# Attention score products of two neighbouring heads in two row tiles of the TensorE array

## What is computed

```python
q, k_text, v_text = hidden @ Wq, text @ Wk, text @ Wv
logits = einsum('bhqd,bhkd->bhqk', q_h, k_h) * scale          # 77 text tokens
text_out = softmax(logits) @ v_h
scores = einsum('bhqd,bhkd->bhqk', q_h, ip_k_h) * scale       # 179 ip tokens
fused = scores + 0.5 * sem[:, None]                           # sem: one for all heads
ip_out = (softmax(fused) * spatial_mask) @ ip_v_h
out = (text_out + ip_out) @ Wout + bout + residual
```

## Time and profile before

| | |
|---|---|
| median of 3 runs | 1717.98 us (1716.74 to 1719.43) |
| the profiled execution | 1715.15 us |
| its span, first to last instruction | 1713.0 us |
| granted TensorE clock, mean | 0.988 |
| PE busy | 1625.4 us, 95% |
| DVE busy | 1380.9 us, 81% |
| ACT busy | 1033.4 us, 60% |
| POOL busy | 833.2 us, 49% |

### The profile page before, as it was taken

One profiled execution on the slowest core, in us unless ns is written; L12 is line 12 of the kernel. 1 busy time (PEld: TensorE's weight loads), 2 busy tenths in 40 slices (PEclk: granted clock), 3 DMA queues, 4 the chain that ended last, 5 costly groups with the idle time before them and its releaser, 6 DMA issues.

```text
span 1713.0 us, 42882 instructions
## 1 busy us (share of the span) xinstructions
PE 1625.4 (95%) x14568; PEld 1440.6 (84%) x14568; DVE 1380.9 (81%) x3630; ACT 1033.4 (60%) x2204; POOL 833.2 (49%) x691
## 2 busy tenths in 40 slices
PE   4899999999999999999999999999999999999986
PEld 4788888888888888877888888898889888898965
DVE  4577777777777777866889988999889999999884
ACT  3366665666665666655666666666666666666652
POOL 4422222222222222333577667766677566756663
PEclk9999999999999999998999999999999999999998
DMA  7433343334333433543233323332333223332211
GB/s 204 99 105 109 116 122 112 120 117 122 115 116 114 121 113 117 152 118 90 82 96 100 99 65 87 104 97 81 85 98 103 80 72 97 108 87 55 83 29 41
DMA packets 185985, 172.72 MB, mean 101 GB/s; under 512 B 25760, under 2 KB 185770, under 8 KB 185770
## 3 DMA queue, kind: packets, MB, share of 16 engines
q1 hardware_dynamic: 185770, 169.98, 34.1%
HBM read 110.17 MB, written 57.76 MB: 98 GB/s over the span
## 4 chain that ended last, share of the span: by engine, by line
PE 78%; DVE 9%; ACT 4%; issue 4%; POOL 2%; SPq 2%; DMA 1%; DVEq 0%; ACTq 0%; POOLq 0%
PE MISC L101 25%; PE GP L101 16%; PE NAT L226 9%; PE TR L256 7%; PE PV L303 4%; PE PV L287 4%; PE PV L284 2%; PE PV L306 2%; PE MISC L335 2%; DVE PM L819 2%; DVE TA L806 1%; PE MISC L476 1%; ACT PVS L541 1%; PE PV L244 1%; ACT PH L534 1%
## 5 line engine op out<-in xcount | busy, mean ns | idle before, releaser
L970 POOL TENSOR_TENSOR ZS<-ZP 128x256 f32<-128x256 f32 x267 | 267.2, 1001 | 230.7 <-DVE ZP L813 230.6
L527 ACT ACTIVATE P<-TA 128x512 f32<-128x512 f32 x320 | 202.0, 631 | 269.4 <-DVE TA L806 269.0
L226 PE MATMUL NAT<-KS,QS 65*128 65x256 f32 x1280 | 295.6, 313 | 9.5 <-DMA KS<-qk_parts 5.7
L256 PE MATMUL TR<-QS,KS 69*128 69x256 f32 (+1 forms) x1280 | 272.0, 294 | 0.3 <-DVE TA L806 0.2
L975 POOL TENSOR_TENSOR PARTS<-QKF,PARTS 112x512 fp32r<-112x512 f32 (+3 forms) x96 | 126.7, 1320 | 293.6 <-ACT PARTS L555 293.6
L226 PEld LDWEIGHTS NAT<-KS,QS 65*128 65x128 f32 x1280 | 203.0, 191 | 73.5 <-issue 63.5
L101 PE MATMUL GP<-PH,GH 128*128 128x256 f32 (+1 forms) x960 | 244.2, 285 | 15.9 <-DVE ZP L813 15.9
L813 DVE TENSOR_TENSOR ZP<-GP,PM 128x512 f32<-128x512 f32 x320 | 219.2, 685 | 46.5 <-PE GP L101 43.8
L819 DVE SCALAR_TENSOR_TENSOR PM<-P,PH 128x512 f32<-128x512 f32 x320 | 252.3, 788 | 0.0
L797 DVE TENSOR_REDUCE MX<-NAT 128x2 f32<-128x504 f32 x320 | 216.0, 675 | 33.2 <-PE NAT L226 30.4
L101 PE MATMUL GP<-PH,GL 128*128 128x256 f32 (+1 forms) x960 | 240.9, 279 | 0.0
(11 more groups left out here) (279 smaller groups left out, 3959.9 us busy)
## 6 DMA issues: line engine op xcount, KB each, us to landing
QS<-qk_parts SPq DMA_DIRECT2D x480, 64.0 KB
KS<-qk_parts SPq DMA_DIRECT2D x480, 64.0 KB
qk_parts<-PARTS SPq DMA_DIRECT2D x128, 224.0 KB, 2.8
CT<-in_ctx_t SPq DMA_DIRECT2D x32, 512.0 KB, 4.2
qk_parts<-PARTS SPq DMA_DIRECT2D x64, 192.0 KB, 2.4
QS<-NH SPq DMA_DIRECT2D x480, 4.0 KB
XT<-in_x_t SPq DMA_DIRECT2D x48, 112.0 KB, 2.2
XT<-x_t SPq DMA_DIRECT2D x48, 112.0 KB, 2.3
```

Of the source, the lines that this page charges most:

```text
L226: ins = e.matmul(NAT[s % 2][:, i * T:(i + 1) * T], QS[0:KQ, h, i * 128:(i + 1) * 128], KS[0:KQ, h, :], start=True, stop=True)
L256: ins = e.matmul(TR[s % 2][:, i * S:(i + 1) * S], KS[0:w, h, i * 128:(i + 1) * 128], QS[0:w, h, :], start=True, stop=True)
L527: e.activation(P[:, s % NP, :], TA[:, s % 2, :], ACT.Exp, scale=SCALE).then_inc(q["exp"], 1)
L970: e.tensor_tensor(ZS[s % NZ][:, :], ZP[:, s % 2, 0:S], ZP[:, s % 2, S:2 * S], ALU.add).then_inc(q["zs"], 1)
```

## The change

It is one rewrite of how scores are stacked, multiplied and read:

- The stacks lose their zero rows and are 48 rows high (`KM`); even heads stand in rows 0 to 47 of QS and KS, odd heads in rows 64 to 111 (`UP`), the rows of maxima and ones right behind each. Both are 10 pairs wide for each of two batches.
- NAT and TR are one tile each of two banks; a pair of heads is multiplied by four matmuls into each, by turns in the lower and the upper row tile (64 rows by 128 columns of the array). On PE, TR and NAT of a pair stand next to each other at the end of every second slot, NAT 10 slots ahead instead of 11.
- DVE reads a pair's maxima in one reduction (in layer 0 the four passes of the fused term stay), TA, PM, P and PH are made for two heads in one instruction.
- `spill` writes the parts to DRAM in the order of the stack, three times 16 rows for Q and for K; `stack` fetches half a batch with four DMAs. The rows of maxima go to DRAM with one DMA and from there to QS with two.
- The offsets of other work, and the rule by which the ring hands out banks, are changed: each taker says how long it will hold its bank, and the bank that comes free first is taken.

```diff
-KQ, KM = 65, 65
-STACKS = 2 * len(Q_PARTS)
-LEAD = 11
+KM, UP = 48, 64
+LEAD = 10
+HP = H // 2
...
+STACK = ((-1, 3), (7, 11))
...
 def mrows(g):
 
-    return 64 * (g // 2 + 1) if g < G1 else 32 * G1 + 32 * ((g - G1) // 2 + 1)
+    return 32 * (g // 2 + 1)
 
...
-    QS, KS = sb("QS", [TRK0, H, S], F32R), sb("KS", [TRK0, H, T], F32R)
+    QS, KS = sb("QS", [UP + TRK0, 2 * HP, S], F32R), sb("KS", [UP + TRK0, 2 * HP, T], F32R)
...
-    NAT = [bank(f"NAT{k}") for k in range(2)]
-    TR = [bank(f"TR{k}") for k in range(2)]
+    NAT, TR = (ctx.enter_context(nc.psum_tensor(n, [128, 1024], F32)) for n in ("NAT", "TR"))
...
+    def pair_at(t, off, lo=0, hi=2 * S1):
+
+        return t - off if (t - off) % 2 == 0 and lo <= t - off < hi else None
+
+    def slot_of(s):
+
+        return s // H % 2 * HP + s % H // 2
...
-            s = t + LEAD
-            if 0 <= s < 2 * S1:
-                b, h = divmod(s, H)
-                if s == 0:
-                    e.wait_ge(q["w_rest"], 3 * 16)
-                    e.wait_ge(q["clear"], 4)
-                    e.wait_ge(q["clear_q"], 2)
-                if h % HG == 0:
-                    e.wait_ge(q[f"stack{h // HG}"], stacked(b + 1))
-                if s >= 2:
-                    e.wait_ge(q["mx"], s - 1)
-                for i in range(2):
-                    ins = e.matmul(NAT[s % 2][:, i * T:(i + 1) * T], QS[0:KQ, h, i * 128:(i + 1) * 128],
-                                   KS[0:KQ, h, :], start=True, stop=True)
-                ins.then_inc(q["nat"], 1)
...
+            s = pair_at(t, 0)
+            if s is not None:
+                b, h, k = s // H, s % H, slot_of(s)
+                if h % HG == 0:
+                    e.wait_ge(q[f"mrow{s // HG % 2}"], mrows(s // HG))
+                    if s == 0:
+                        e.wait_ge(q["sel"], 32)
+                if s:
+                    e.wait_ge(q["sum"] if s <= S1 else q["exp"], s // 2)
+                w = TRK0 if b < B else TRK1
+                for i in range(2):
+                    for r in (0, UP):
+                        ins = e.matmul(TR[:, 8 * r + i * S:8 * r + (i + 1) * S], KS[r:r + w, k, i * 128:(i + 1) * 128],
+                                       QS[r:r + w, k, :], start=True, stop=True)
+                ins.then_inc(q["tr"], 1)
+            s = pair_at(t, -LEAD)
+            if s is not None:
+                b, h, k = s // H, s % H, slot_of(s)
+                if s == 0:
+                    e.wait_ge(q["w_rest"], 3 * 16)
+                if h % HP == 0:
+                    e.wait_ge(q[f"stack{h // HP}"], stacked(h // HP, b + 1))
+                if s:
+                    e.wait_ge(q["mx"], s // 2)
+                for i in range(2):
+                    for r in (0, UP):
+                        ins = e.matmul(NAT[:, 8 * r + i * T:8 * r + (i + 1) * T], QS[r:r + KM, k, i * 128:(i + 1) * 128],
+                                       KS[r:r + KM, k, :], start=True, stop=True)
+                ins.then_inc(q["nat"], 1)
 
...
+            s = pair_at(t, 2, 0, S1)
+            if s is not None:
                 if s == 0:
                     e.wait_ge(q["once"], 2)
                     e.wait_ge(q["norm"], 1)
                     e.wait_ge(q["vall_out"], 16)
                 if s >= NP and s % HG == 0:
                     e.wait_ge(q["pv"], (s - NP) // HG + 1)
-                if s < S1:
-                    e.wait_ge(q["sum"], s + 1)
-                    e.activation(P[:, s % NP, :], TA[:, s % 2, :], ACT.Exp, scale=SCALE).then_inc(q["exp"], 1)
-                else:
-                    e.wait_ge(q["tr"], s + 1)
-                    e.activation(P[:, s % NP, :], TR[s % 2][:, :], ACT.Exp, scale=SCALE).then_inc(q["exp"], 1)
-                    if s - S1 >= NS:
-                        e.wait_ge(q["gp"], s - S1 - NS + 1)
-                    e.wait_ge(q["exp"], s + 1)
-                    e.copy(PH[:, s % NS, :], P[:, s % NP, :]).then_inc(q["ph"], 1)
-            for off, lo, hi, width in ((HG + 1, 0, G1, 2 * S), (HG + 3, G1, 2 * G1, S)):
+                e.wait_ge(q["sum"], s // 2 + 1)
+                e.activation(P[:, s % NP:s % NP + 2, :], TA[:, :, :], ACT.Exp, scale=SCALE).then_inc(q["exp"], 1)
+            s = pair_at(t, 1, S1)
+            if s is not None:
+                if s % HG == 0:
+                    e.wait_ge(q["pv"], (s - NP) // HG + 1)
+                e.wait_ge(q["tr"], s // 2 + 1)
+                e.activation(P[:, s % NP:s % NP + 2, :], TR[:, :].rearrange("p (r n) -> p r n", r=2), ACT.Exp, scale=SCALE).then_inc(q["exp"], 1)
+                k = (s - S1) % NS
+                if s - S1 >= NS:
+                    e.wait_ge(q["gp"], s - S1 - NS + 2)
+                e.wait_ge(q["exp"], s // 2 + 1)
+                e.copy(PH[:, k:k + 2, :], P[:, s % NP:s % NP + 2, :]).then_inc(q["ph"], 1)
+            for off, lo, hi, width in ((HG + 2, 0, G1, 2 * S), (HG + 4, G1, 2 * G1, S)):
                 g = due_group(t, off, lo, hi)
...
+            s = pair_at(t, 1, 0, S1)
+            if s is not None:
+                b, h = divmod(s, H)
+                if h == 0:
+                    e.wait_ge(q["st"], b + 1)
+                if s:
+                    e.wait_ge(q["exp"], s // 2)
+                e.wait_ge(q["tr"], s // 2 + 1)
+                e.tensor_tensor(TA[:, :, :], TR[:, :].rearrange("p (r n) -> p r n", r=2),
+                                ST[:, b % 2, :].unsqueeze(1).broadcast_to([128, 2, 2 * S]), ALU.add).then_inc(q["sum"], 1)
+            s = t - 3 - S1
+            if 0 <= s < S1:
+                if s >= 2:
+                    e.wait_ge(q["zs"], s - 1)
+                e.wait_ge(q["pm"], s // 2 + 1)
+                e.wait_ge(q["gp"], s + 1)
+                e.tensor_tensor(ZP[:, s % 2, :], GP[:, :], PM[:, s % 2, :], ALU.mult).then_inc(q["zp"], 1)
+            s = pair_at(t, 1 - LEAD)
+            if s is not None:
+                b, h = divmod(s, H)
+                g, j = s // HG, s % HG // 2
+                v = NAT[:, :].rearrange("p (r a t) -> p a r t", r=2, a=2)
+                m = MX[:, g % 2, :, :].rearrange("p a (g r q) -> p a g r q", g=2, r=2)
+                if j == 0 and g >= 2:
+                    e.wait_ge(q["mxt"], g - 1)
+                if s:
+                    e.wait_ge(q["mx"], s // 2)
+                e.wait_ge(q["nat"], s // 2 + 1)
+                if s < S1:
+                    e.tensor_reduce(m[:, :, 0, :, j], v[:, :, :, 0:NT0], AX.X, ALU.max)
+                    if h == 0:
+                        e.wait_ge(q["sn"], b + 1)
+                    for r in range(2):
+                        for i in range(2):
+                            ins = e.tensor_tensor_reduce(TMP[:, r, i, :], v[:, i, r, NT0:T], SN[:, b % 2, i, :], 1.0, -3.0e38, ALU.add, ALU.max,
+                                                         MX[:, g % 2, i, HG + 2 * r + j:HG + 2 * r + j + 1])
+                    ins.then_inc(q["mx"], 1)
+                else:
+                    e.tensor_reduce(m[:, :, 0, :, j], v[:, :, :, 0:NT], AX.X, ALU.max).then_inc(q["mx"], 1)
+            s = pair_at(t, 2, S1)
+            if s is not None:
+                k = (s - S1) % NS
+                if s > S1:
+                    e.wait_ge(q["zp"], s - S1)
+                e.wait_ge(q["ph"], (s - S1) // 2 + 1)
+                e.scalar_tensor_tensor(PM[:, :, :], P[:, s % NP:s % NP + 2, :], 2.0, PH[:, k:k + 2, :].bitcast(F32), ALU.mult,
+                                       ALU.subtract).then_inc(q["pm"], 1)
             for n, off in enumerate(AT1["gl"]):
...
         def spill(b, m):
             m0, mn = MT[m]
             e.wait_ge(q["qk_lo"], 3 * b + m + 1)
-            for i in range(2):
-                e.dma_start(parts_h[b % 2, i, :, m0:m0 + mn, :].rearrange("j r t -> r j t"),
-                            PARTS[0:mn, m, :, i * S:(i + 1) * S].bitcast(F32)).then_inc(q[f"spilled{m}"], 16)
-
-        def stack(b, hg):
-            h0, h1 = HG * hg, HG * hg + HG
-            for r in range(len(Q_PARTS)):
-                for i, dst, parts in ((0, QS, Q_PARTS), (1, KS, K_PARTS)):
-                    e.dma_start(dst[16 * r:16 * r + 16, h0:h1, :].bitcast(F32),
-                                parts_h[b % 2, i, parts[r], D * h0:D * h1, :].rearrange("(h d) t -> d h t", d=D)).then_inc(q[f"stack{hg}"], 16)
+            for i, parts in ((0, Q_PARTS), (1, K_PARTS)):
+                for r in range(3):
+                    e.dma_start(parts_h[b % 2, i, D * r:D * r + D, m0 // D:(m0 + mn) // D, :].rearrange("d h t -> h d t"),
+                                PARTS[0:mn, m, parts[r], i * S:(i + 1) * S].bitcast(F32)).then_inc(q[f"spilled{m}"], 16)
+
+        def stack(b, half):
+            k = b % 2 * HP + half * HP // 2
+            for r in range(2):
+                for i, dst in ((0, QS), (1, KS)):
+                    e.dma_start(dst[UP * r:UP * r + KM, k:k + HP // 2, :].bitcast(F32),
...
-            g = due_group(t, -4 * HG)
+                if g >= 2:
```

(29 more changed lines are left out.)

228 lines of the change are left out of this document (78 added, 150 removed).

## The result

The changed kernel takes **1913.8 us** (median of 4 runs, 1912.9 to 1923.0) against 1718.0 us (1716.7 to 1719.4): 1.115 times as long, 95% interval 1.112 to 1.119. I had forecast 1695, with a range of 1595 to 1738. The profiled execution has a span of 1912.2 us.

A forecast was written before the change was run, and what follows sets the result against it. PE was taken to set the pace nearly everywhere, with DVE just behind in layer 1. Terms -35 - 3 + 10 + 5 = -23 us gave 1692 for the profiled execution, forecast as a 1695 us median; range 1595 to 1738.

The forecast's parts named there:

- Score products: On PE, side-by-side row tiles save 0.48 us a pair, less 0.37 for switching: 0.11 x 320 pairs, -35 us.
- DVE and ACT merges: Merged instructions take 26 us of work per layer off DVE and shrink ACT's; neither sets the pace, so worth nothing.
- Queues: On SP's DMA queue, fewer DMAs but more spills, and maxima through DRAM; everything lands in time, so costed at nothing.
- The prediction's own test: PE waits for max_rows or qk_parts DMAs would prove the zero for the queues wrong.
- New waits: Single pair buffers: layer 0's NAT waits in two pairs a batch, +10 us; layer 1's DVE falls behind, +5 us.
- Rival 3: Single buffers eat the gain: DVE's maximum late in many pairs, 0.15 us in each of 320, 1728 us; chance 0.17.

The follow-up runs named there:

- d2: Against a 1820.1 us version with row tiles and layer 0's Q a slot earlier: layer 1's PM made per head again, ACT waiting for PM; 1850.7 us.
- a1: Changed kernel with the spills and DRAM layout of the kernel before, each half stack then being twelve moves of 16 rows; 1816.2 us.
- b5: Kernel before with the changed kernel's six spill DMAs per tile in place of its own two; 1843.8 us.
- b1: a1 with the transposes of the maxima behind TR and NAT on PE, and NH behind TA on DVE; 1815.7 us.
- best version: b1 plus layer 0's maxima rows moved directly, layer 1's first half stack a slot earlier, layer 0's V at 6, 8, 17; 1791.4 us (median of four), ratio 1.045.
- c1: a1 with the rows of maxima moved straight from NH to QS in layer 0 alone, without DRAM; 1801.7 us.
- e2: First single execution of the best version, which moved layer 0's V products to 6, 8, 17 against a 1786.3 us version; 1784.5 us.
- b4: a1 with a pair's TR and NAT products issued head by head instead of by turns between row tiles; 1821.5 us.

## Why the prediction was wrong

I forecast 1695 us and the kernel takes 1914. The step that failed is the zero for the queues; two more terms were too small or missing.

- **Score products, -35 us**: right as a reading of the timeline, to 0.01 us in an undisturbed visit; no run took the row tiles out alone.
- **DVE and ACT merges, 0**: DVE lost 66 us of work (I had 52) and ACT 56. No run prices them; d2, which undid one of them, was slower and not faster.
- **Queues, 0**: this step failed. I counted DMAs and bytes ("still less than what is left before the TR") and not SP's time for an issue by its shape, nor what stands behind it. 18 spills a batch of 0.75 us in blocks of six, then a stack that waits for them to land (6.0 us), then the next group's rows. I gave the first leg of the maxima 4.5 us; SP stood 85 times of 160 until it had landed, up to 6.0 us. In the changed kernel this is 98 us net by a1, and in the kernel before the same spills cost 129 (b5). The prediction's own test (PE waits for max_rows or qk_parts prove the zero wrong) came out: 47.4 and 44.7 us over the span. The total was no warning either: SP issues for 25.6 us in a batch of layer 0 after, 32.0 before. What counts is how long a block is and what waits behind it.
- **New waits, +10 and +5**: right in kind, too small in size, and in the wrong place. For layer 0 I took two pairs in ten and 0.3 us; PE waits 20 times in 500 us, which is two in a batch, but 1.3 us each (25.3 us). Rival 3, many pairs with 0.15 us each, is not what the waits show. In layer 1 I took 0.3 us a batch more for ZP; PE waits 21.6 us for it in 700 us against 1.0 before, 1.8 a batch more. I had placed the wait of layer 0 at NAT and overlooked that the transposes of the maxima (L467) stand ahead of TR in the new order: every fourth slot all of PE waits for the maxima 0.5 us earlier than NAT needs them, and DVE idles (78.3 us in that window) for ACT's NH. Moving the transposes (b1) gave nothing, though.
- **The clock**: not in the prediction. Before, PE was busy 98% and its granted clock 1.00 in both layers; now stalls of some us are followed by stretches at 1.2 GHz. No run had the waits without it, but its size can be bounded. Over the span the granted clock fell from 0.988 to 0.935; 6.5% of 1912 us less 1.2% of 1713 are 104 us. As an estimate, then, up to half of the loss is the lower level that the stalls brought, and the rest the stalls themselves; some of those 104 us fell where PE idled or would have waited anyway. By the same sum it is up to 52 of a1's 101 us, and in the best version (0.964) 44 of 74.
- **The start and the change of layers**: not in the prediction. They are +20 and +43 us after, +14 and +31 in a1. No experiment went there, so how much of it is the clock, the half stacks or the tables stays open.

The sum in a1, with spills as before: +18 in ten batches of layer 0, +27 in layer 1, +31 between, +14 at the start, +8 in the first three batches, +3 at the end, 101 in all. The steps from c1 to e2 gave back some 30 of it. Of the 68 to 74 us that the best version is behind, I have shown places (light pairs, ZP and small handovers of 0.4 to 0.8 us in layer 1), and not that they are all.

## What to carry to other kernels

Price a DMA by its issue time on the queue that issues it, by shape, from a row of the same shape, and then read the queue's order: a block of issues is a delay for everything behind it, and a wait for a landing is a longer one. A change that takes away a second buffer turns an average (4.5 us of PE a pair against 2.9 of DVE) into a condition on each single pair. Where TensorE ran full at the upper clock, put a price on what follows a stall too: here up to as much again as the stalls.

## What the runs showed of the hardware

- Row tiles of 48 to 52 rows: couples within 0.005 us in the visit shown and 0.012 in all undisturbed ones, 0.12 us a step for 256 columns, weight loads of 128 columns together; each change of the array's division costs about 0.18 us in and 0.18 out.
- Written head by head or by turns, eight products of two row tiles take the same 0.22 us to the second couple and 0.67 us a visit (b4).
- An issue of a spill of 16 rows of 7 heads took 0.75 us on SP, one of 112 rows in two parts 0.38, a move of two or four heads' rows from NH to one row of QS 0.56 and 0.58, a DMA of 512 bytes 0.25 (medians).
- 1152 idle DMAs on SP (0.6 MB, 312 us of issues) cost 104 us, with no landing slower; the granted clock in layer 0 fell from 1.00 to 0.91.
